# The counting of edges per node in a graph block: which one-hot is stationary and which one moves

## The chip, the core and the metric

One Trainium2 chip, one of its cores. The metric is the device time of one execution of the program in microseconds (us), the median over several runs.

## What is computed

The reference puts four blocks behind one another on 8192 rows of 128 numbers: a leaky attention over a dense adjacency matrix, a graph block with a list of edges and four experts, a second dense attention, and a routed mixture of eight experts. The change touches only the preparation of the second block, in which edges are sorted by the node that they lead to:

```
src = concatenate([edge_index[0], loops]); dst = concatenate([edge_index[1], loops])
e_max = segment_max(e, dst, num_segments=M)
denom = segment_sum(ee, dst, num_segments=M)
agg = segment_sum(msg, dst, num_segments=M)
```

The list has 524288 edges. To sort them by `dst`, the kernel first counts how many edges lead to each of the 8192 nodes.

## The kernel before, in words

The program is a chain of phases; each phase is a block in which every engine has its own instruction list, and a block ends when all engines have ended theirs. The first three phases are in `sort_and_project`. "pack" reads the edges and squeezes the wanted ones to the left of each of 128 partitions; "count" (lines 626 to 711) counts them per node; "place" (from line 714) gives each edge its place in the sorted list. The attention follows.

A node number is written as 64 * part + offset: part is one of P = 128, offset one of NF = 64. The edges stand in columns of 128, one edge on each partition. A group is GC = 8 columns. For a group, VectorE builds two arrays of ones and zeros in bf16 with `one_hots_across` (lines 932 to 935): the offset one-hots OF (128 partitions x 64 x 8; first instruction, line 934) and the part one-hots OP (128 x 128 x 8; second instruction, line 935). The group's column number is the innermost index of both arrays, so that `OF[:, :, c]`, one column's one-hots, is a read of 64 elements that lie 8 bf16 elements, 16 bytes, apart, and `OP[:, :, c]` one of 128 elements that lie 16 bytes apart.

TensorE then multiplies, for each of the 8 columns, one one-hot against the other and adds the product to one table in PSUM. The table has an entry for every pair (part, offset). There are two tables, counted one after the other: HISTC from OPC and OFC (edges of one special source, loop at lines 695 to 700, 112 groups in the profiled execution) and HIST from OP and OF (the other edges, loop at lines 703 to 708, 38 groups). Before and behind each loop a matmul with a tile `zero` opens or closes the accumulation (lines 694, 701, 702, 709). No matmul is left out for an empty column.

The order is held by semaphores. The one-hots have two buffers. VectorE may build group g when the matmuls of group g - 2 have ended (`counted`, `same_counted`); TensorE may start on group g when its second one-hot is built (`hot`, `same_hot`). The opening matmul adds 2 to `counted`, so that VectorE can't build for the second table before the first one is closed. Behind the loops VectorE copies HISTC to `repeat` (line 671), adds 1 to HIST for the loop edge of each node (line 674), sums it (line 675), gets a prefix over the partitions through one TensorE matmul (line 711) and works out the starts of the nodes' ranges. Beside this, SyncE's queue clears the tensor `runs` in DRAM (line 651); ScalarE does nothing and GpSimd only one memset.

In the phase "place" four kinds of matmul matter for the reading of the rows. Line 872 adds the product of `OP[b][:, :, c]` (stationary) and `OF[b][:, :, c]` (moving) to a table, with the same spacing of elements as in "count". Line 849 has the stationary `OP[b][:, :, c]` with 16 bytes between elements, and the moving 128 x 128 identity, whose elements are adjacent. Lines 855 and 856 have a broadcast column stationary and adjacent elements moving, and accumulate in pairs on one place in PSUM.

Of the kernel before, what the change touches and what calls it, by code (L numbers as in the profile page):

```python
# [8 lines left out]
ALU = mybir.AluOpType  # L9
# [9 lines left out]
P = 128  # L19
BANK = 512  # L20
# [219 lines left out]
def sort_and_project(nc, ident, edge_index, N, rec, plan, self_idx, self_rec, ctl, endi, cont, repeat, runs,  # L240
# [14 lines left out]
    NF = N // P  # L255
# [10 lines left out]
    with Phase(nc, "sort") as ph:  # L266
# [356 lines left out]
        with Phase(nc, "count") as pc:  # L623
            OF = [pc.sbuf(f"OF{k}", [P, NF, GC], BF16) for k in range(2)]
            OP = [pc.sbuf(f"OP{k}", [P, P, GC], BF16) for k in range(2)]
            w = pc.sbuf("w", [P, 8, NF])
            wi = pc.sbuf("wi", [P, NF], I32)
            tot = pc.sbuf("tot", [P, 2])
            zero = pc.sbuf("zero", [P, P], BF16)
            OFC = [pc.sbuf(f"OFC{k}", [P, NF, GC], BF16) for k in range(2)]  # L630
            OPC = [pc.sbuf(f"OPC{k}", [P, P, GC], BF16) for k in range(2)]
            HIST = pc.psum("hist", [P, BANK])
            HISTC = pc.psum("histc", [P, BANK])
            BASE = pc.psum("base", [P, BANK])
            hot, counted, hist_ok, tot_ok, base_ok, dve_step, zero_ok = pc.sems(
                "hot", "counted", "hist_ok", "tot_ok", "base_ok", "dve_step", "zero_ok")
            same_hot, same_counted, same_ok = pc.sems("same_hot", "same_counted", "same_ok")
            runs_clear, runs_out = pc.sems("runs_clear", "runs_out")
            clear = pc.sbuf("clear", [P, CHUNK, runs.shape[1]])
            HC = CE // 2  # L640
            with nc.Block() as block:
                @block.gpsimd
                def _(pool):
                    nc.gpsimd.memset(clear[:], 0.0).then_inc(runs_clear, 1)

                @block.sync
                def _(sp):
                    rows = runs.rearrange("(p t) c -> p t c", p=P)
                    sp.wait_ge(runs_clear, 1)
                    with sp.Fori(0, LMAX // CHUNK) as i:  # L650
                        sp.dma_start(rows[:, bass.ds(i * CHUNK, CHUNK), :], clear[:]).then_inc(runs_out, 16)
                    sp.wait_ge(runs_out, 16 * (LMAX // CHUNK))

                @block.vector
                def _(dve):
                    groups = dve.value_load(ctl[0:1, 0:1], min_val=1, max_val=CE // (2 * GC))
                    same_groups = dve.value_load(ctl[0:1, 3:4], min_val=1, max_val=HC // GC)
                    nc.vector.memset(zero[:], 0.0).then_inc(zero_ok, 1)
                    with dve.Fori(0, same_groups) as i:
                        for b in range(2):  # L660
                            dve.wait_ge(same_counted, 2 * i + b + 1)
                            cols = bass.ds(i * GC + b * HC, GC)
                            one_hots_across(nc, OFC[b], OPC[b], value, offC[:, cols], partC[:, cols], NF, GC)[1].then_inc(same_hot, 1)
                    with dve.Fori(0, groups) as i:
                        for b in range(2):
                            dve.wait_ge(counted, 2 * i + b + 1)
                            cols = bass.ds((2 * i + b) * GC, GC)
                            one_hots_across(nc, OF[b], OP[b], value, offB[:, cols], partB[:, cols], NF, GC)[1].then_inc(hot, 1)
                    step = Chain(dve, dve_step)
                    dve.wait_ge(same_ok, 1)  # L670
                    step(nc.vector.tensor_copy(repeat[:], HISTC[:, 0:NF]))
                    dve.wait_ge(hist_ok, 1)
                    c1, incl, start, last = w[:, 0, :], w[:, 1, :], w[:, 2, :], w[:, 3, :]
                    step(nc.vector.tensor_scalar(c1, HIST[:, 0:NF], 1.0, None, ALU.add))
                    step(nc.vector.tensor_reduce(tot[:, 0:1], c1, AX.X, ALU.add))
                    dve.sem_inc(tot_ok, 1)
                    dve.wait_ge(base_ok, 1)
                    step(nc.vector.tensor_copy(tot[:, 1:2], BASE[:, 0:1]))
                    step(nc.vector.tensor_tensor_scan(incl, c1, c1, tot[:, 1:2], ALU.add, ALU.max))
                    step(nc.vector.tensor_tensor(start, incl, c1, ALU.subtract))  # L680
                    step(nc.vector.tensor_scalar(start1[:], start, 1.0, None, ALU.add))
                    step(nc.vector.tensor_scalar(last, incl, -1.0, None, ALU.add))
                    step(split_rows(nc, step, start, Lc[:, 0:1], Lc[:, 1:2], Lc[:, 2:3], Lc[:, 3:4], wi[:], w[:, 4, :], w[:, 5, :], w[:, 6, :], self_idx[:]))
                    step(split_rows(nc, step, last, Lc[:, 0:1], Lc[:, 1:2], Lc[:, 2:3], Lc[:, 3:4], wi[:], w[:, 4, :], w[:, 5, :], w[:, 6, :], endi[:]))

                    step(nc.vector.scalar_tensor_tensor(out=w[:, 7, :], in0=w[:, 6, :], scalar=Lc[:, 2:3], in1=start, op0=ALU.mult, op1=ALU.add))
                    step(nc.vector.tensor_scalar(cont[:], w[:, 7, :], 0.0, None, ALU.is_lt))

                @block.tensor
                def _(pe):  # L690
                    groups = pe.value_load(ctl[0:1, 0:1], min_val=1, max_val=CE // (2 * GC))
                    same_groups = pe.value_load(ctl[0:1, 3:4], min_val=1, max_val=HC // GC)
                    pe.wait_ge(zero_ok, 1)
                    nc.tensor.matmul(HISTC[:, 0:NF], zero[:], zero[:, 0:NF], start=True, stop=False, skip_group_check=True).then_inc(same_counted, 2)
                    with pe.Fori(0, same_groups) as i:
                        for b in range(2):
                            pe.wait_ge(same_hot, 2 * i + b + 1)
                            for c in range(GC):
                                ins = nc.tensor.matmul(HISTC[:, 0:NF], OPC[b][:, :, c], OFC[b][:, :, c], start=False, stop=False, skip_group_check=True)
                            ins.then_inc(same_counted, 1)  # L700
                    nc.tensor.matmul(HISTC[:, 0:NF], zero[:], zero[:, 0:NF], start=False, stop=True, skip_group_check=True).then_inc(same_ok, 1)
                    nc.tensor.matmul(HIST[:, 0:NF], zero[:], zero[:, 0:NF], start=True, stop=False, skip_group_check=True).then_inc(counted, 2)
                    with pe.Fori(0, groups) as i:
                        for b in range(2):
                            pe.wait_ge(hot, 2 * i + b + 1)
                            for c in range(GC):
                                ins = nc.tensor.matmul(HIST[:, 0:NF], OP[b][:, :, c], OF[b][:, :, c], start=False, stop=False, skip_group_check=True)
                            ins.then_inc(counted, 1)
                    nc.tensor.matmul(HIST[:, 0:NF], zero[:], zero[:, 0:NF], start=False, stop=True, skip_group_check=True).then_inc(hist_ok, 1)
                    pe.wait_ge(tot_ok, 1)  # L710
                    nc.tensor.matmul(BASE[:, 0:1], tri[:], tot[:, 0:1], start=True, stop=True).then_inc(base_ok, 1)


        with Phase(nc, "place") as pp:
            OF = [pp.sbuf(f"OF{k}", [P, NF, GC], BF16) for k in range(2)]
            OP = [pp.sbuf(f"OP{k}", [P, P, GC], BF16) for k in range(2)]
# [215 lines left out]
def one_hots_across(nc, off_hot, part_hot, value, off, part, NF, GC):  # L932

    return (nc.vector.tensor_tensor(off_hot[:], value[:, 0:NF, :], off.unsqueeze(1).to_broadcast([P, NF, GC]), ALU.is_equal),
            nc.vector.tensor_tensor(part_hot[:], value[:], part.unsqueeze(1).to_broadcast([P, P, GC]), ALU.is_equal))
# [1851 lines left out]
def graph_network(nc, x, adj, L0_gnn_W, L0_gnn_a, L0_ffn_W_gat, L0_ffn_att_src, L0_ffn_att_dst, L0_ffn_b_gat,  # L2787
# [28 lines left out]
    with Phase(nc, "top") as top:  # L2816
# [12 lines left out]
        low = top.sbuf("low", [P, 1])  # L2829
        levels = top.sbuf("levels", [1, 1], I32)  # L2830
        sort_and_project(nc, ident, L0_ffn_edge_index, N, rec, plan, self_idx, self_rec, ctl, endi, cont, repeat, runs,
                         x, L0_gnn_W, L0_gnn_a, H, rows0, WD, srow, scol, dcol, low, levels)
        wide = top.sbuf("X", [P, T + 4, D])
# [40 lines left out]
```

## Time and profile before

| what | value |
|---|---|
| median of three runs | 4454.92 us |
| lowest and highest | 4442.82 and 4462.66 us |
| span of the profiled execution, first to last instruction | 4090.2 us |
| median of the runs minus that span | 364.7 us |
| phase "count", first matmul to the last one of the loops | 414.7 to 597.6 us of the span |

The profiled execution's time with what lies around it was not recorded apart; its span is all of it that the profile gives. All changes of a phase are therefore worked out within the span and added to the median of the runs.

The page of the profile gives for each engine its busy time, and in 40 slices of about 102 us how busy it was. PE is TensorE's matmuls, PEld its loads of stationary operands, DVE VectorE. In the lists of instructions, "128*128 128x64" on a matmul means 128 rows by 128 columns of stationary operand and 64 moving columns. The ends of matmuls are modelled, so the distance from start to start is the better measure of what a matmul costs in a stream.

### The profile page before, as it was taken

How to read it: one execution, taken by the hardware profiler on the slowest of the kernel's cores; microseconds unless marked ns; L12 is line 12 of the kernel's file. 1: busy time of each engine (PE TensorE's matmuls, PEld its weight loads, DVE VectorE, ACT ScalarE, POOL GpSimd, SP SyncE). 2: the span in 40 equal slices, each digit the busy share in tenths (PEclk: the TensorE clock that was granted, in tenths of full speed). 3: DMA queues.
4: the chain of work that ended last, by engine and by line, in shares of the span. 5: the costliest groups of instructions: out<-in, count | busy, mean ns of one | idle time of the engine just before them, and what ended most of it. 6: DMA issues, size and time to landing. Idle time of an engine off the chain costs nothing. (4 is left out here: it accounts for less than half of the span.)

```text
span 4090.2 us, 62225 instructions
## 1 busy us (share of the span) xinstructions
PE 2990.8 (73%) x17446; PEld 1902.2 (47%) x17446; DVE 2628.1 (64%) x5711; ACT 1614.7 (39%) x2876; POOL 1166.2 (29%) x1158
## 2 busy tenths in 40 slices
PE   0300879839999999999954887101599999977994
PEld 0300768725555555555533555001466666644663
DVE  9999779968888888888884222237734444442333
ACT  5301005527777777777753555101400010012221
POOL 0000005047777400000002777760001211213442
PEclk9999999969999999999985999555599999988997
DMA  3200940058878878777741222133233333323446
GB/s 136 72 0 0 371 163 12 0 195 281 290 273 288 294 269 288 284 279 289 282 145 22 73 73 69 33 96 103 98 102 108 114 103 108 113 63 125 129 124 187
DMA packets 278617, 619.23 MB, mean 151 GB/s; under 512 B 74673, under 2 KB 117816, under 8 KB 277374
## 3 DMA queue, kind: packets, MB, share of 16 engines
q1 hardware_dynamic: 211446, 502.44, 37.0%
q10 hardware_dynamic: 32200, 92.89, 5.7%
q0 software_dynamic: 34880, 22.97, 2.9%
q14 instruction: 68, 0.56, 0.0%
q8 instruction: 23, 0.38, 0.0%
HBM read 434.17 MB, written 185.82 MB: 152 GB/s over the span
## 5 line engine op out<-in xcount | busy, mean ns | idle before, releaser
L1749 PE MATMUL at_out<-at_pt,top_H 128*128 128x512 f32 x2048 | 995.1, 608 | 54.7 <-DVE at_turned L1669 46.4
L1591 ACT ACTIVATE at_rl<-at_qrow,at_less,at_steep 128x512 f32<-128x512 f32 x1024 | 746.5, 805 | 8.7 <-DVE at_turned L1669 8.6
L1973 PE MATMUL at_out<-at_parts,at_a 128*128 128x387 bf16 x4096 | 686.1, 328 | 15.7 <-DVE at_parts L2046 15.7
L1676 DVE SCALAR_TENSOR_TENSOR at_pt<-at_rl,at_turned 128x1024 f32<-128x1024 f32 x512 | 608.9, 1218 | 15.7 <-ACT at_rl L1591 15.7
L1973 PEld LDWEIGHTS at_out<-at_parts,at_a 128*128 128x128 fp8e4 x4096 | 399.7, 98 | 289.0 <-issue 17.9
L1669 DVE CAST at_turned<-at_tp 128x1024 uint8<-128x1024 f32 x322 | 393.5, 1222 | 172.7 <-PE at_tp L1740 170.7
L1749 PEld LDWEIGHTS at_out<-at_pt,top_H 128*128 128x128 f32 x2048 | 349.3, 191 | 309.3 <-issue 301.8
L1740 PEld LDWEIGHTS at_tp<-at_identS,at_adj 128*128 128x128 fp8e4 x4128 | 274.9, 98 | 302.2 <-issue 302.2
L921 POOL DMA_INDIRECT rec<-at_part x304 | 381.6, 1255 | 103.7 <-issue 85.9
L1073 POOL DMA_INDIRECT runs_GT<-tab,runs_RC x352 | 338.3, 961 | 115.9 <-issue 105.5
L1740 PE MATMUL at_tp<-at_identS,at_adj 128*128 128x128 bf16 x4128 | 316.1, 220 | 9.1 <-DMA at_adj<-in_adj_dram 8.4
L1921 POOL DMA_INDIRECT slots<-at_Y,at_dest x128 | 123.5, 965 | 634.0 <-DVEq L2151 597.9
L1598 ACT CAST at_turned<-at_tp 128x1024 uint8<-128x1024 f32 x192 | 193.8, 1009 | 223.3 <-PE at_tp L1740 223.3
L1065 POOL DMA_INDIRECT runs_firstg<-tab,runs_firsti x2 | 2.0, 985 | 828.3 <-DVEq L1092 828.0
L2424 PE MATMUL ex_hp<-ex_XS,ex_WB 128*128 128x512 f32 (+1 forms) x472 | 217.2, 596 | 1.9 <-DMA ex_WB<-wts 1.9
L2530 POOL DMA_INDIRECT y<-ex_YS,ex_to x156 | 151.5, 971 | 201.3 <-DVE ex_YS L2511 161.5
L1128 DVE TENSOR_TENSOR runs_own<-runs_GT,runs_flag 128x64 f32<-128x64 f32 x22 | 6.8, 308 | 312.5 <-DMA runs_GT<-tab,runs_RC 312.5
L2008 ACT ACTIVATE at_small<-at_small 128x4 f32<-128x4 f32 x16 | 3.3, 205 | 500.8 <-DVEq L2104 500.8
L2490 DVE TENSOR_TENSOR ex_HH<-ex_SU,ex_hp 128x512 f32<-128x512 f32 (+1 forms) x118 | 80.8, 685 | 163.2 <-ACT ex_SU L2468 163.2
L2468 ACT ACTIVATE ex_SU<-ex_hp 128x512 f32<-128x512 f32 (+1 forms) x118 | 70.4, 596 | 235.1 <-PE ex_hp L2424 235.1
L1227 PEld LDWEIGHTS runs_yp<-runs_down,runs_HH 128*128 128x128 f32 x1024 | 144.9, 219 | 17.8 <-issue 15.6
L1216 PE MATMUL runs_hp<-top_H,runs_up 128*128 (+1 forms) x256 | 125.9, 616 | 30.4 <-DVEq L1110 30.4
(591 smaller groups left out, 4470.4 us busy)
## 6 DMA issues: line engine op xcount, KB each, us to landing
at_adj<-in_adj_dram SPq DMA_DIRECT2D x516, 512.0 KB
adjT<-at_turned ACTq DMA_DIRECT2D x128, 512.0 KB, 5.2
at_a<-adjT SPq DMA_DIRECT2D x128, 512.0 KB, 3.6
runs<-count_clear SPq DMA_DIRECT2D x131, 384.0 KB, 4.0
ex_WB<-wts SPq DMA_DIRECT2D x42, 533.0 KB, 3.6
y<-runs_YS ACTq DMA_DIRECT2D x65, 256.0 KB, 2.1
f_YB<-y SPq DMA_DIRECT2D x16, 1024.0 KB, 11.4
ex_SL<-slots SPq DMA_DIRECT2D x42, 260.0 KB, 3.6
```

The lines of the kernel that those rows point to most:

```text
L921: pool.indirect_dma_start(rec, bass.IndirectOffsetOnAxis(ap=part[h][:, c, 2:3], axis=0), part[h][:, c, 0:2], None, bounds_check=LAST, oob_ ...
L1073: pool.indirect_dma_start(GT[b][:, c, :], None, tab, bass.IndirectOffsetOnAxis(ap=RC[b][:, c, 1:2], axis=0)).then_inc(gt_in[b], 16)
L1227: ins = nc.tensor.matmul(YP[:, x % 2, q * D:(q + 1) * D], HH[x % 2][k][:, q * P:(q + 1) * P], down[:, x, k, :], start=False, stop=(q == GQ ...
L1591: ins = nc.scalar.activation(RL[v % NBUF][:, k, :], qrow[:], ACT.Relu, bias=less[:], scale=steep[:, u:u + 1])
L1598: nc.scalar.copy(AT[c % NAT][:, 2 * (v % VC):2 * (v % VC) + 2, :], TP[v % 2][:]).then_inc(copied[0], 1)
L1669: nc.vector.tensor_copy(AT[c % NAT][:, 2 * (v % VC):2 * (v % VC) + 2, :], TP[v % 2][:]).then_inc(copied[1], 1)
L1676: nc.vector.scalar_tensor_tensor(out=PT[v % NBUF][:], in0=RL[v % NBUF][:], scalar=1.0, in1=AT[v // VC % NAT][:, 2 * (v % VC):2 * (v % VC) ...
L1740: ins = nc.tensor.matmul(TP[v % 2][:, k, t * P:(t + 1) * P], bits[c % NBUF][:, t, o:o + P, 0], identS[:], start=True, stop=True)
L1749: ins = nc.tensor.matmul(OUT[:], H[:, u, :], PT[v % NBUF][:, k, :], start=(u == 0), stop=(u == T - 1))
L1973: ins = nc.tensor.matmul(OUT[:, g, x, 0:3 * D1], ones[c % NBUF][:, j, x * P:(x + 1) * P], parts[:, u].rearrange("p k d -> p (k d)"), start ...
L2424: ins = nc.tensor.matmul(HP[0:n, k, s, :], WB[b][:, w:w + n], XS[b][:], start=True, stop=True)
L2530: pool.indirect_dma_start(y, bass.IndirectOffsetOnAxis(ap=to[b][:, q:q + 1], axis=0), YS[b][:, q, :], None, bounds_check=2 * N - 1, oob_is ...
```

## The change

In both loops and in the four opening and closing matmuls the operands change places. The offset one-hots (64 columns) become stationary, the part one-hots (128 columns) move. The tables lie on 64 partitions by 128 columns in place of 128 by 64. At the end each table is copied to SBUF (`lying`), turned by a TensorE transpose into a new PSUM tile (`TURN`), and read from there. Two semaphores for each way are added. The builds on VectorE, the groups, the buffers and their waits stay.

```diff
+            TURN = pc.psum("turn", [P, 2, BANK])
+            lying = pc.sbuf("lying", [NF, 2, P])
+            lies, stands = [pc.sem(f"lies{k}") for k in range(2)], [pc.sem(f"stands{k}") for k in range(2)]
...
                     dve.wait_ge(same_ok, 1)
-                    step(nc.vector.tensor_copy(repeat[:], HISTC[:, 0:NF]))
+                    nc.vector.tensor_copy(lying[:, 0, :], HISTC[0:NF, 0:P]).then_inc(lies[0], 1)
                     dve.wait_ge(hist_ok, 1)
+                    nc.vector.tensor_copy(lying[:, 1, :], HIST[0:NF, 0:P]).then_inc(lies[1], 1)
+                    dve.wait_ge(stands[0], 1)
+                    step(nc.vector.tensor_copy(repeat[:], TURN[:, 0, 0:NF]))
+                    dve.wait_ge(stands[1], 1)
                     c1, incl, start, last = w[:, 0, :], w[:, 1, :], w[:, 2, :], w[:, 3, :]
-                    step(nc.vector.tensor_scalar(c1, HIST[:, 0:NF], 1.0, None, ALU.add))
+                    step(nc.vector.tensor_scalar(c1, TURN[:, 1, 0:NF], 1.0, None, ALU.add))
...
                             for c in range(GC):
-                                ins = nc.tensor.matmul(HISTC[:, 0:NF], OPC[b][:, :, c], OFC[b][:, :, c], start=False, stop=False, skip_group_check=True)
+                                ins = nc.tensor.matmul(HISTC[0:NF, 0:P], OFC[b][:, :, c], OPC[b][:, :, c], start=False, stop=False, skip_group_check=True)
...
-                    nc.tensor.matmul(HISTC[:, 0:NF], zero[:], zero[:, 0:NF], start=False, stop=True, skip_group_check=True).then_inc(same_ok, 1)
-                    nc.tensor.matmul(HIST[:, 0:NF], zero[:], zero[:, 0:NF], start=True, stop=False, skip_group_check=True).then_inc(counted, 2)
+                    nc.tensor.matmul(HISTC[0:NF, 0:P], zero[:, 0:NF], zero[:], start=False, stop=True, skip_group_check=True).then_inc(same_ok, 1)
+                    nc.tensor.matmul(HIST[0:NF, 0:P], zero[:, 0:NF], zero[:], start=True, stop=False, skip_group_check=True).then_inc(counted, 2)
...
                             for c in range(GC):
-                                ins = nc.tensor.matmul(HIST[:, 0:NF], OP[b][:, :, c], OF[b][:, :, c], start=False, stop=False, skip_group_check=True)
+                                ins = nc.tensor.matmul(HIST[0:NF, 0:P], OF[b][:, :, c], OP[b][:, :, c], start=False, stop=False, skip_group_check=True)
...
-                    nc.tensor.matmul(HIST[:, 0:NF], zero[:], zero[:, 0:NF], start=False, stop=True, skip_group_check=True).then_inc(hist_ok, 1)
+                    nc.tensor.matmul(HIST[0:NF, 0:P], zero[:, 0:NF], zero[:], start=False, stop=True, skip_group_check=True).then_inc(hist_ok, 1)
+                    for k in range(2):
+                        pe.wait_ge(lies[k], 1)
+                        nc.tensor.transpose(TURN[:, k, 0:NF], lying[:, k, :], ident[0:NF, 0:NF]).then_inc(stands[k], 1)
```

## Rows read from the trace of the kernel before

**Rows 1.** Windows of "count": us, busy us of each engine (instructions), granted clock, DMA share, GB/s.

```profile
414.50:551.00 136.50, 119.55 (x897) 102.13 (x898) 110.75 (x225) 0.00 (x0) 0.00 (x0) 1.00 0.97 378
551.00:598.00 47.00, 41.11 (x309) 34.66 (x307) 38.13 (x77) 0.00 (x0) 0.00 (x0) 1.00 0.00 0
```

**Rows 2.** Waits between 415 and 600 us: us in total, times, longest.

```profile
DVE count_OFC L934 <- PE count_histc L699: 24.2, 55, 0.5
PE count_histc L699 <- DVE count_OPC L935: 16.7, 56, 1.3
```

**Rows 3.** Timeline of two pairs of groups: start us, us, engine, line, xcount, idle before.

```profile
450.02 2.14 PE L699 MATMUL count_histc<-count_OFC,count_OPC 128*128 128x64 bf16 x16 [0.29 <-DVE count_OPC L935]
...
451.35 0.43 DVE L934 TENSOR_TENSOR count_OFC<-sort_value,sort_both 128x512 bf16<-128x512 bf16 x1 [0.45 <-PE count_histc L699]
451.70 0.68 DVE L935 TENSOR_TENSOR count_OPC<-sort_value,sort_both 128x1024 bf16<-128x1024 bf16 x1
452.30 0.43 DVE L934 TENSOR_TENSOR count_OFC<-sort_value,sort_both 128x512 bf16<-128x512 bf16 x1
...
452.44 0.81 PE L699 MATMUL count_histc<-count_OFC,count_OPC 128*128 128x64 bf16 x5 [0.28 <-DVE count_OPC L935]
```

**Rows 4.** Instructions on the two tables: ns min/median/max, first and last start in us.

```profile
L699 PE MATMUL count_histc<-count_OFC,count_OPC x896: 293/302/327, 416.2 to 550.9; 128*128 128x64 bf16 x180
L707 PE MATMUL count_hist<-count_OF,count_OP x304: 293/302/325, 552.6 to 597.6; 128*128 128x64 bf16 x152
```

**Rows 5.** Timeline of the passage from the first table to the second.

```profile
551.05 0.23 PE L701 MATMUL count_histc<-count_zero 128*128 128x64 bf16 x1
551.10 0.23 PE L702 MATMUL count_hist<-count_zero 128*128 128x64 bf16 x1
```

**Rows 6.** Timeline of the start of "place", stationary read at 16 bytes, moving elements adjacent.

```profile
612.08 1.07 PE L849 MATMUL place_tb<-place_identB,place_OP 128*128 128x128 bf16 x8 [5.21 <-DVE place_OP L775]
```

**Rows 7.** Line 849 up to 616.2 us and behind it: ns min/median/max, starts.

```profile
L849 PE MATMUL place_tb<-place_identB,place_OP x8: 311/311/323, 612.1 to 612.8; 128*128 128x128 bf16 x8
L849 PE MATMUL place_tb<-place_identB,place_OP x304: 219/226/236, 616.4 to 808.7; 128*128 128x128 bf16 x152
```

**Rows 8.** Line 872 up to 616.2 us and behind it: ns min/median/max, starts.

```profile
L872 PE MATMUL place_hr<-place_OF,place_OP x3: 297/301/316, 614.6 to 616.0; 128*128 128x64 bf16 x3
L872 PE MATMUL place_hr<-place_OF,place_OP x300: 287/316/322, 616.0 to 809.5; 128*128 128x64 bf16 x150
```

**Rows 9.** Timeline of TensorE in "place" at 614 and at 700 us.

```profile
614.43 0.31 PE L855 MATMUL place_dd<-place_identF,sort_partB 128*128 128x128 bf16 x1
614.54 0.31 PE L856 MATMUL place_dd<-place_identB,sort_offB 128*128 128x128 bf16 x1
614.65 0.30 PE L872 MATMUL place_hr<-place_OF,place_OP 128*128 128x64 bf16 x1
614.77 0.62 PE L876 MATMUL place_lk<-place_HS,place_OPT 128*128 128x64 f32 x2
...
699.79 0.42 PE L849 MATMUL place_tb<-place_identB,place_OP 128*128 128x128 bf16 x4
700.07 0.31 PE L872 MATMUL place_hr<-place_OF,place_OP 128*128 128x64 bf16 x1
...
700.41 0.22 PE L855 MATMUL place_dd<-place_identF,sort_partB 128*128 128x128 bf16 x1
700.46 0.22 PE L856 MATMUL place_dd<-place_identB,sort_offB 128*128 128x128 bf16 x1
```

**Rows 10.** Timeline of the end of "count".

```profile
595.74 2.14 PE L707 MATMUL count_hist<-count_OF,count_OP 128*128 128x64 bf16 x16 [0.26 <-DVE count_OP L935]
...
596.57 0.22 DVE L671 COPY top_repeat<-count_histc 128x64 f32<-128x64 f32 x1
...
597.71 0.23 PE L709 MATMUL count_hist<-count_zero 128*128 128x64 bf16 x1
598.05 0.23 DVE L674 TENSOR_SCALAR count_w<-count_hist 128x64 f32<-128x64 f32 x1 [1.26 <-PE count_hist L709]
598.31 0.22 DVE L675 TENSOR_REDUCE count_tot<-count_w 128x1 f32<-128x64 f32 x1
...
598.64 0.58 PE L711 MATMUL count_base<-count_tot,sort_tri 128*128 128x1 f32 x2 [0.70 <-DVEq L676]
599.27 0.16 DVE L678 COPY count_tot<-count_base 128x1 f32<-128x1 f32 x1 [0.73 <-PE count_base L711]
```

**Rows 11.** Two single f32 transposes: a stationary operand of 64 and of 128 columns.

```profile
L610 PEld LDWEIGHTS pack_st<-top_ident,top_scol x1: 129/129/129, 310.6 to 310.6; 128*64 128x64 f32 x1
L610 PE MATMUL pack_st<-top_ident,top_scol x1: 422/422/422, 310.6 to 310.6; 128*64 128x128 f32 x1
L587 PEld LDWEIGHTS pack_ms<-top_ident,sort_both x1: 182/182/182, 11.8 to 11.8; 128*128 128x128 f32 x1
```

More of the change, by code:

```diff
@@ L693, in _ @@
                     pe.wait_ge(zero_ok, 1)
-                    nc.tensor.matmul(HISTC[:, 0:NF], zero[:], zero[:, 0:NF], start=True, stop=False, skip_group_check=True).then_inc(same_counted, 2)
+                    nc.tensor.matmul(HISTC[0:NF, 0:P], zero[:, 0:NF], zero[:], start=True, stop=False, skip_group_check=True).then_inc(same_counted, 2)
                     with pe.Fori(0, same_groups) as i:
```

## Prediction, made before the changed kernel ran

> **What bounds the kernel now.** I read the page's slices first, to find when the edited lines run, and then looked only at "count". The windows show it as some 183 us in which ScalarE and GpSimd do nothing and neither TensorE nor VectorE is busy all the time: 119.6 and 110.8 us of the first 136.5 us [rows 1]. The only DMA there clears a tensor and has ended before the second table is counted, where the share falls from 0.97 to 0.00 [rows 1]; a phase ends when its slowest engine does, so that every microsecond added to the counting is added to the span.
>
> The waits show that the two engines wait for each other in turn, once in each pair of groups (55 and 56 times) [rows 2]. The timeline shows why. In the pair shown, TensorE starts at 450.02 and issues 16 matmuls in 2.14 us; the last one lasts 0.302 us [rows 4], so that starts are (2.14 - 0.302) / 15 = 0.1225 us apart, call it 0.12 us [rows 3]. The eighth starts at 450.02 + 7 x 0.12 = 450.86 and ends at about 451.16; VectorE's next build starts at 451.35, some 0.2 us later, lasts until 451.70 + 0.68 = 452.38, and TensorE goes on at 452.44 [rows 3]. So the pair's period of 2.42 us is the round trip of one buffer: build 1.03 + signal 0.06 + matmuls 0.84 + 0.30 + signal 0.19 = 2.42. TensorE alone would need 16 x 0.12 = 1.92 us. VectorE alone would need 2 x 0.95 = 1.90 us, from its starts at 451.35 and 452.30 [rows 3]. The kernel runs 56 + 19 = 75 such pairs. The two loops last from 416.2 to 551.05 and from 552.56 to 597.71 us, together 134.8 + 45.2 = 180.0 us [rows 4, 5, 10].
>
> **What a matmul costs here.** The change halves the stationary columns and doubles the moving ones, so everything hangs on which of the two sets the 0.12 us. I compared four kinds of matmul.
>
> First, 64 moving columns of adjacent elements: the closing and opening matmuls start 0.05 us apart and last 0.23 us [rows 5]. The counting ones, with 64 moving columns 16 bytes apart, take 0.12 us and last 0.302 us: about 0.07 us more in each measure. So adjacent reading runs at 0.05 / 64 = 0.8 ns a column, and the difference must come from the operands' spacing, stationary or moving.
>
> Second, a stationary operand of 128 columns 16 bytes apart, with 128 adjacent moving columns (line 849): eight matmuls in 1.07 us, so (1.07 - 0.311) / 7 = 0.108 us apart [rows 6, 7]. That is what 128 adjacent moving columns cost at that time, whatever the stationary operand is, for lines 855 and 856, with a broadcast column, are 0.11 us apart too [rows 9]. Later on the same line is (0.42 - 0.226) / 3 = 0.065 us apart [rows 7, 9]. So a load of 128 spaced columns needs at most 0.065 us, half of the 0.12 us, and hides behind a matmul.
>
> Third, line 872, which has the operands of the counting. It lasts 301 ns up to 616.2 us and 316 ns behind it, while line 849 falls from 311 to 226 ns [rows 7, 8]. The next matmul starts 0.12 us after it [rows 9], although it stands alone and nothing of its own kind is before or behind it. So this is no hazard of accumulating on one PSUM place again and again (lines 855 and 856 accumulate in pairs 0.05 us apart at 700.41 [rows 9]), and it isn't paced by TensorE's clock. What is left is the reading of the moving operand: about 0.12 us for 64 elements, 1.9 ns for each.
>
> On the clock: between 614 and 700 us, with no change of form, the distance of lines 855 and 856 falls from 0.11 to 0.05 us [rows 9], the ratio of the two levels of 1.2 and 2.4 GHz. The granted clock is given as 1.00 throughout "count" [rows 1], but the 0.23 us of the opening matmul's 64 columns against 0.226 us for 128 columns at 700 us [rows 5, 7] fit the lower level; I take that record as silent before 616 us. For my sum it does not matter, since line 872 shows that the spaced read is no faster at the higher level.
>
> The Trainium skill has a rule on this ("SBUF — State Buffer", in its note on cachelines): lines are of 16 bytes, and reads that go to a new line each time are penalised, which for bf16 begins at a step of 8 elements. That is this layout, the trace agrees (0.12 against 0.05 us), and it speaks against the change, for the change makes the longer of the two spaced operands the moving one. The rule that speaks for it is in "TensorE: Matmul & The Clock Gate", section "LDWEIGHTS (loading the stationary operand)": a load takes its columns / 1.2 ns, 107 ns for 128 and 53 ns for 64, by which 0.12 us would be mostly the load. The 0.065 us of line 849 speaks against that. The same page ties the fast load of weights to 128 of them, so that the new load of 64 loses it; by the page that load is then 53 ns.
>
> **The sum, part by part.**
>
> 1. Moving columns from 64 to 128, all spaced: start to start from 0.12 to 2 x 0.12 = 0.24 us, and the duration from 0.30 to 0.42 us. Bounds: from below, of the 0.302 us only what exceeds the in-stream matmul's fixed part counts as read; that part is 311 - 107 = 204 ns for line 849 [rows 7, 9], which leaves 98 ns for 64 columns, 1.53 ns each, and 0.196 us for 128. From above, line 872 at the higher clock: 316 - (226 - 65) = 155 ns, 2.4 ns a column, 0.31 us for 128. I take 0.24 because the stream itself, the nearest row, shows it without any fixed part taken off.
>
> 2. The stationary operand from 128 to 64 columns: its load is hidden now and stays hidden behind 0.24 us. No row has a 64-column bf16 load; an f32 one takes 129 against 182 ns [rows 11]. Even at 1.9 ns a column, 0.12 us, it is covered. Value: nothing. Were it not covered, it would cost up to 0.12 us each (third rival).
>
> 3. The loop. The round trip of a buffer becomes 1.03 + 0.06 + 7 x 0.24 + 0.42 + 0.19 = 3.38 us, but TensorE alone needs 16 x 0.24 = 3.84 us for a pair. So TensorE becomes the bound, and VectorE, done 0.46 us ahead, waits for it. Each pair takes 3.84 us in place of 2.42 (2.40 on the mean). All 1200 matmuls: 1200 x 0.24 = 288.0 us in place of 180.0: **+108.0 us**. VectorE's 150 builds don't change, and nothing else is in the phase to be covered by the longer loops: the clearing DMA ends earlier than them.
>
> 4. Openings and closings, each table: the last matmul's drain is 0.12 us longer. Twice: +0.2 us.
>
> 5. The turn at the end. The second table's chain gets a copy from PSUM, about 0.25 us (128x64 takes 0.22 us [rows 10]; this one is 64x128), and a trip to TensorE and back with an f32 transpose: between 598.53, where the sum on line 675 ends, and 599.27 the like trip takes 0.74 us with 0.58 us of matmul [rows 10], against 0.42 us for a single transpose [rows 11]. So 0.25 + 0.74 + a little for the second semaphore: +1.0 us. The first table's copy and transpose, and the copy to `repeat` (0.22 us), lie within these waits; the copy to `repeat`, queued on VectorE ahead of line 674, waits only for the first transpose, which TensorE does before the second table's copy is done. Bounds of this part: 0.7 to 1.5 us.
>
> Sum: 108.0 + 0.2 + 1.0 = **+109 us**. The span goes from 4090.2 to about 4199 us. The median of the runs lies 364.7 us above the span, and nothing in the change touches what is around it: 4454.9 + 109 = **4564 us**, 2.4% slower. By the bounds of part 1 the loops need 1200 x 0.196 = 235 us (TensorE's 3.14 us a pair is then hardly above the round trip of 3.04) or 1200 x 0.31 = 372 us: +56 and +193 us with parts 4 and 5, that is 4511 and 4648 us.
>
> **The rivals.**
>
> First: the load sets the pace, and the moving spaced read costs little. Then the halved load goes away as the bound and matmuls are paced by 128 columns at 0.107 us with a duration of 0.311 us as on line 849 [rows 7]. The round trip: 1.03 + 0.06 + 0.75 + 0.31 + 0.19 = 2.34 us against 2.42. That is -0.08 x 75 = -6 us, +1 us for the turn: 4450 us, within the noise. For it: the counting's loads and matmuls both have spaced operands, and no row has a spaced moving operand with an adjacent stationary one. Against it: line 849's 0.065 us with the same load. It needs a load of over 0.107 us. If in addition the clock went to its higher level (distance 0.05, duration 0.22 [rows 9]), the round trip would be 1.03 + 0.06 + 0.35 + 0.22 + 0.19 = 1.85 us, VectorE's 1.90 us would bound, and (2.40 - 1.90) x 75 = 37 us would be won: 4419 us. This is the case that ends on the other side.
>
> Second: loads and moving reads share one supply of spaced reads. 128 + 64 = 192 elements cost 0.12 us now, and 64 + 128 = 192 cost the same after: nothing but the turn, 4456 us. For it: 0.12 / 192 gives 0.63 ns, and line 849's 0.065 us for 128 spaced elements gives 0.5 ns, not far from it. Against it: line 872 has its next load beside it in adjacent f32 and still takes 0.12 us.
>
> Third: the new load of 64 columns isn't hidden: it comes at 0.12 us (1.9 ns a column) on top of the 0.24. Then 1200 x 0.36 = 432 us, +253 us: 4708 us. Against it: loads hide now in every stream that I looked at. It decides only if spaced reads of both operands exclude each other, which the 0.12 us of today leaves no room for at 0.065 + 0.12.
>
> That the change doesn't do what it says isn't likely: the operands are exchanged in both loops, and nothing depends on data.
>
> **How the numbers follow.** Forecast 0.82; first rival 0.06 within its 6 us and 0.03 with the faster clock; second 0.04; third 0.05. The median of the three runs scatters by some 20 us, so 0.5% (22 us) is about what can be told from no change. Slower by more than that: 0.82 + 0.05 = 0.87. Same: 0.06 + 0.04 = 0.10. Faster: 0.03. The range holds the forecast with nearly the whole of part 1's bounds, 4510 to 4640; the rivals outside have 0.18 together.
>
> **What would show it.** In the profile after, lines 699 and 707 (moved down by a few lines) should be 0.24 us apart and last about 0.42 us; TensorE should have no idle time in the loops except at their starts, and VectorE should wait for it some 1.9 us in each pair, in both groups; the stretch from the first to the last counting matmul should be near 290 us; the time from the last closing matmul to line 675's successor should be 1 us longer. A distance near 0.12 us would show the second rival, 0.107 us or less the first, 0.36 us the third. I am wrong if the distance does not scale with the moving columns, or if the spaced read is slowed today by the load beside it and gets faster with the smaller one.

## The result, and the profile after

| | before | after | ratio, 95% interval |
|---|---|---|---|
| median, first comparison | 4448.87 us | 4539.88 us | 1.0232 [1.0191, 1.0273] |
| median, second comparison (a faster chip) | 4095.21 us | 4194.81 us | 1.0235 [1.0206, 1.0265] |

The changed kernel is slower by 91 us between the medians of the first comparison, by 0.0232 x 4448.87 = 103 us by its ratio, and by 99.6 us in the second. Neither interval holds 1. The prediction was +109 us, 4564 us.

Windows of the counting in the changed kernel (columns as in [rows 1]):

```profile
414.50:622.00 207.50, 206.18 (x896) 174.09 (x897) 114.88 (x224) 0.00 (x0) 0.00 (x0) 1.00 0.64 248
622.00:694.00 72.00, 70.77 (x309) 59.41 (x307) 39.09 (x77) 0.00 (x0) 0.00 (x0) 1.00 0.00 0
```

TensorE is busy for 206.2 of 207.5 us, where it was for 119.6 of 136.5 [rows 1]. VectorE is busy for 154.0 us over both windows, where it was for 148.9. The waits, over both loops, now have one direction:

```profile
DVE count_OFC L944 <- PE count_histc L706: 90.0, 110, 1.4
DVE count_OF L944 <- PE count_hist L714: 29.8, 36, 1.4
...
PE count_histc L706 <- DVE count_OPC L945: 1.3, 1, 1.3
PE count_hist L714 <- DVE count_OP L945: 1.2, 1, 1.2
```

TensorE waits once for each table, at its start. VectorE waits before 110 groups of 112 and 36 of 38, 0.82 us each time. Before, each engine waited once in a pair [rows 2]. The instructions on the first table, and where the loops end:

```profile
L706 PE MATMUL count_histc<-count_OPC,count_OFC x896: 405/409/481, 416.1 to 622.0; 128*64 128x128 bf16 x180
...
L708 PE MATMUL count_histc<-count_zero x1: 287/287/287, 622.3 to 622.3; 128*64 128x128 bf16 x1
```

A matmul lasts 409 ns instead of 302 [rows 4]. From 416.1 to 622.3 us are 206.2 us for 896 matmuls: 0.230 us from start to start. The second table takes from 623.9 to 693.9 us, 70.0 us for 304, the same pace. The loops take 276.2 us in place of 180.0: +96 us. The end of the phase, from the timeline:

```profile
693.86 0.29 PE L716 MATMUL count_hist<-count_zero 128*64 128x128 bf16 x1
694.07 0.18 PEld L719 LDWEIGHTS count_turn<-top_ident,count_lying 64*128 64x128 f32 x1 [0.29 <-issue]
694.07 0.81 PE L719 MATMUL count_turn<-top_ident,count_lying 64*128 64x64 f32 x2
694.18 0.28 DVE L676 COPY count_lying<-count_hist 64x128 f32<-64x128 f32 x1 [2.46 <-PE count_hist L716]
694.48 0.23 DVE L678 COPY top_repeat<-count_turn 128x64 f32<-128x64 f32 x1
...
695.00 0.23 DVE L681 TENSOR_SCALAR count_w<-count_turn 128x64 f32<-128x64 f32 x1 [0.30 <-PE count_turn L719]
```

From the closing matmul's start to the instruction that adds 1 are 1.14 us, where it was 598.05 - 597.71 = 0.34 [rows 10]: the turn costs 0.8 us. The passage from the first table to the second takes 623.87 - 622.25 = 1.62 us in place of 1.51. Together: +97 us within "count".

### The profile page after: what moved, and what is told of

It is laid out like the page before. It is cut to its first block and busy times, and to the rows that moved or that the text cites. A ratio compares the mean times of both kernels' runs of the same rounds, so it can differ in the third digit from the quotient of the medians.

```text
span 4558.5 us, 62231 instructions
## 1 busy us (share of the span) xinstructions
PE 3214.6 (71%) x17448; PEld 2075.7 (46%) x17448; DVE 2633.6 (58%) x5713; ACT 1613.0 (35%) x2876; POOL 1132.4 (25%) x1158
## 5 line engine op out<-in xcount | busy, mean ns | idle before, releaser
L1759 PE MATMUL at_out<-at_pt,top_H 128*128 128x512 f32 x2048 | 1015.1, 619 | 95.4 <-DVE at_turned L1679 48.8
L931 POOL DMA_INDIRECT rec<-at_part x304 | 355.8, 1170 | 103.7 <-issue 95.2
L1152 DVE TENSOR_TENSOR runs_sum_in<-runs_GT,runs_sum_in 128x256 f32<-128x256 f32 x22 | 17.2, 783 | 431.1 <-ACT runs_decay L1175 412.1
L706 PE MATMUL count_histc<-count_OPC,count_OFC 128*64 128x128 bf16 x896 | 206.3, 409 | 1.3 <-DVE count_OPC L945 1.3
L706 PEld LDWEIGHTS count_histc<-count_OPC,count_OFC 128*64 128x64 bf16 x896 | 174.0, 194 | 33.4 <-DVE count_OPC L945 1.4
L1226 PE MATMUL runs_hp<-top_H,runs_up 128*128 (+1 forms) x256 | 142.5, 670 | 52.6 <-DVEq L1120 30.4
```

Of the source, the lines that this page charges most:

```text
L706: ins = nc.tensor.matmul(HISTC[0:NF, 0:P], OFC[b][:, :, c], OPC[b][:, :, c], start=False, stop=False, skip_group_check=True)
L931: pool.indirect_dma_start(rec, bass.IndirectOffsetOnAxis(ap=part[h][:, c, 2:3], axis=0), part[h][:, c, 0:2], None, bounds_check=LAST, oob_ ...
L1759: ins = nc.tensor.matmul(OUT[:], H[:, u, :], PT[v % NBUF][:, k, :], start=(u == 0), stop=(u == T - 1))
```

## The experiments

The theory: in these loops a matmul's pace is set by the reading of its moving operand, whose elements are 16 bytes apart. The change doubles that operand. The rivals: the load of the stationary operand sets the pace; both reads share one supply; part of the loss comes elsewhere. Except where noted, an experiment changes only the counting.

**The kernel before, unchanged.** The profiled executions of before and after differ by 4558.5 - 4090.2 = 468 us, of which only 97 lie in "count".

> The kernel before, unchanged, to see how its parts spread from one profiled execution to the next. Both theories: the two counting loops again take 180 us in all, with 0.12 us from matmul to matmul. The profiled executions of before and after differ by 468 us in span though only 96 us of that lie in the counting; if that rest has nothing to do with the change, this run's span lies near 4450 us rather than at 4090 us, with the phase 'place' near 300 us and the graph block near 540 us as in the profile after. If the rest came with the change, the span is near 4090 us.

This one execution took 4438.73 us, with a span of 4437.0 us. Its counting is that of the first profile: 302 ns, and loops of 135.1 + 45.2 = 180.3 us.

```profile
L699 PE MATMUL count_histc<-count_OFC,count_OPC x896: 293/302/326, 416.3 to 551.3; 128*128 128x64 bf16 x180
```

The rest of the difference lies behind, in the same code. Windows of "place" and of the graph block, first of the first profile of before, then of this run:

```profile
598.00:811.00 213.00, 190.17 (x1850) 161.50 (x1851) 200.18 (x1395) 107.55 (x457) 61.39 (x62) 1.00 0.06 20
2224.00:2564.00 340.00, 263.38 (x1310) 187.18 (x1311) 75.63 (x279) 179.18 (x283) 256.65 (x267) 0.89 0.27 67
```

```profile
598.00:895.00 297.00, 207.47 (x1856) 181.26 (x1854) 201.84 (x1401) 107.40 (x457) 60.06 (x62) 0.80 0.04 14
2359.00:2890.00 531.00, 310.88 (x1309) 202.49 (x1310) 75.04 (x287) 175.62 (x280) 260.14 (x276) 0.76 0.16 43
```

The same instructions take 297 and 531 us in place of 213 and 340. The busy times of VectorE, ScalarE and GpSimd are nearly unchanged; TensorE's grow by 9% and 18%, at a lower granted clock (0.80 in place of 1.00, 0.76 in place of 0.89), and the rest is waiting. The kernel before is thus 9% slower on one chip than on another: its medians were 4479 us on this run's chip and 4095 us on two others. The first profile came from an execution of the latter kind, while its times are of the former. So the 364.7 us that I put "around the span" are nothing of the sort: here time and span differ by 1.7 us. Why these phases depend on the chip was not followed up; the change has no part in it, as the next run shows.

**The changed kernel again, on a chip of the faster kind.**

> The changed kernel once more, beside the kernel before, because the profiled executions of before and after differed by 350 us outside the counting. Theory: the change costs 276 - 180 = 96 us in the loops and 1 us in the turn whatever the rest of the execution is like: 97 us more than the kernel before on the same chip, ratio 1.022 to 1.024. Rival (part of the loss comes later, as a lower granted clock in 'place' that the change brings about): clearly more than 97 us, or another difference where the rest runs faster.

4194.81 against 4095.21 us: +99.6 us, ratio 1.0235 [1.0206, 1.0265]; loops 276.2 us to the tenth. The span of its profile is 4187.2 us, 97.0 us above the 4090.2 of the first profile of before, all of it in "count". The loss is the same where the rest runs 350 us shorter. Its windows behind the counting are those of the first profile of before:

```profile
694.00:909.00 215.00, 191.23 (x1856) 161.87 (x1854) 201.71 (x1407) 107.57 (x457) 61.27 (x62) 1.00 0.06 20
2324.00:2663.00 339.00, 262.74 (x1311) 184.25 (x1312) 75.36 (x279) 179.59 (x284) 255.82 (x268) 0.89 0.26 67
```

**The moving columns cut in two, with 64 stationary ones.**

```diff
-    ins = nc.tensor.matmul(HIST[0:NF, 0:P], OF[b][:, :, c], OP[b][:, :, c], ...)
+    for m in range(2):
+        half_of = slice(m * (P // 2), (m + 1) * (P // 2))
+        ins = nc.tensor.matmul(HIST[0:NF, half_of], OF[b][:, :, c], OP[b][:, half_of, c], ...)
```

> The changed kernel, with each matmul's 128 moving columns cut into two matmuls of 64 columns behind loads of the same 64 stationary columns: twice as many matmuls, the same table. Theory (the spaced moving read sets the pace, 1.68 ns a column, with some 15 ns for each matmul on top): 0.122 us from start to start, the loops at 16 x 2 x 0.122 = 3.90 us a pair, 293 us in all. Proportional to the columns with nothing fixed: 0.115 us, 276 us in all. Rival, the pace of before came from loading 128 spaced columns: 0.06 to 0.10 us, 150 to 240 us in all. Rival, loads and moving reads share one supply (192 elements in 0.12 us): 128 elements, 0.08 us, 192 us in all.

```profile
L708 PE MATMUL count_histc<-count_OPC,count_OFC x1792: 299/299/368, 416.4 to 631.4; 128*64 128x64 bf16 x200
```

1792 matmuls in 631.4 - 416.4 = 215.0 us: 0.120 us each, between the two forms that I had put, with 64 stationary columns, where 128 stationary columns gave 0.1225. Half the load changes the pace by 2%. This ends the first rival (0.06 to 0.10) and the shared supply (0.08). The two loops took 288 us, and the one execution 4603.26 us beside a median of 4479.31 for the kernel before. It also sizes my term: two matmuls of 64 columns take 0.240 us and one of 128 takes 0.230. Read as a straight line, that is 0.010 us for each matmul and (0.230 - 0.120) / 64 = 1.72 ns for each column.

**The moving columns cut in two, in the kernel before.** The same edit, on the kernel before: two matmuls of 32 columns behind 128 stationary ones.

> The kernel before, with each matmul's 64 moving columns cut into two matmuls of 32, each behind a load of the same 128 spaced stationary columns. Theory (1.68 ns a moving column and 15 ns fixed): 0.069 us from start to start if the load of 128 columns, at most 0.065 us on line 849, stays hidden; then a pair's round trip grows by 15 x 0.069 + 0.25 against 7 x 0.122 + 0.30, that is by 0.13 us, the loops take about 190 us in all. Rival, the load of 128 spaced columns sets the pace of before: 0.12 us from start to start still, TensorE alone 3.84 us a pair, 288 us in all.

Timeline of two pairs of groups:

```profile
447.82 2.25 PE L701 MATMUL count_histc<-count_OFC,count_OPC 128*128 128x32 bf16 x32 [0.29 <-DVE count_OPC L939]
450.30 2.26 PE L701 MATMUL count_histc<-count_OFC,count_OPC 128*128 128x32 bf16 x32 [0.23 <-DVE count_OPC L939]
```

(2.25 - 0.24) / 31 = 0.065 us on the mean, as 0.010 + 32 x 1.72 ns = 0.065 gives from the other two sizes. But this mean holds the first step behind each wait, 0.087 to 0.089 us; most of the other steps are 0.060 to 0.067 us, with a median of 0.061, hardly above half of the 0.120 us for 64 columns. So the fixed 0.010 us rests on the step from 64 to 128 columns alone. The loops took 182 us, though every stationary operand is loaded twice; a pace set by the load would have made 288. The one execution took 4472.95 us, 6 us below the median of the kernel before.

**One operand closer at a time.** The arrays are laid out as two blocks of four columns, so that a column's elements are 8 bytes apart; the builds stay two VectorE instructions. The edit shown brings the moving one-hots alone closer; the other array keeps one block of eight columns, 16 bytes from element to element.

```diff
-    OF = [pc.sbuf(f"OF{k}", [P, NF, GC], BF16) for k in range(2)]
+    OF = [pc.sbuf(f"OF{k}", [P, GC // 4, NF, 4], BF16) for k in range(2)]
...
-    ins = nc.tensor.matmul(HIST[:, 0:NF], OP[b][:, :, c], OF[b][:, :, c], ...)
+    ins = nc.tensor.matmul(HIST[:, 0:NF], OP[b][:, c // 8, :, c % 8], OF[b][:, c // 4, :, c % 4], ...)
```

First the moving one-hots alone:

> The kernel before with only the moving one-hots (64 offset columns) laid out 8 bytes apart; the stationary ones stay 16 bytes apart. Theory (the moving read alone sets the pace): 0.055 to 0.065 us from matmul to matmul, loops near 143 to 150 us, VectorE's 1.90 us a pair being the bound. Rival (two spaced operands share one supply of reads, so the spaced load counts too): between 0.065 and 0.12 us, by 0.63 ns for each of the 128 spaced stationary elements 0.08 us or more.

Then the stationary ones alone:

> The kernel before with only the stationary one-hots (128 part columns) laid out 8 bytes apart; the moving ones stay 16 bytes apart. Theory: 0.120 us from matmul to matmul as before, loops 180 us. Rival (the load of 128 spaced columns sets the pace, or shares it): 0.06 to 0.08 us, loops 145 to 155 us.

Timelines, of the moving ones closer (from its second run, below) and of the stationary ones closer:

```profile
448.15 0.71 PE L707 MATMUL count_histc<-count_OFC,count_OPC 128*128 128x64 bf16 x8 [0.23 <-DVE count_OPC L243]
...
449.17 0.72 PE L707 MATMUL count_histc<-count_OFC,count_OPC 128*128 128x64 bf16 x8 [0.31 <-DVE count_OPC L243]
```

```profile
449.21 2.05 PE L707 MATMUL count_histc<-count_OFC,count_OPC 128*128 128x64 bf16 x16 [0.31 <-DVE count_OPC L243]
```

With the moving ones closer, (0.71 - 0.248) / 7 = 0.066 us, 248 ns each. With the stationary ones closer, (2.05 - 0.297) / 15 = 0.117 us, loops of 176 us. So the moving operand's spacing is nearly all of it; the stationary one's costs 0.005 us of the 0.1225. One execution of each gave 4062.6 and 4099.4 us beside a median of 4094.9. The first again, over four executions:

> The kernel before with the moving one-hots alone 8 bytes apart, timed: the loops take 145.6 us, 34 us less than 180; 4 us more than with both 8 bytes apart, if the loads of 16-byte spacing cost anything where the pace is VectorE's. Ratio to the kernel before 0.992.

4060.69 against 4095.21 us, ratio 0.990 [0.9872, 0.9928]. The loops took 145.6 us. Its waits show that VectorE is the bound, for it waits only at the tables' starts, and TensorE before each group:

```profile
PE count_histc L707 <- DVE count_OPC L243: 31.1, 112, 1.3
...
DVE count_OF L243 <- PE count_hist L710: 1.0, 1, 1.0
```

**Both operands closer, in the kernel before.**

> The kernel before with the one-hots of both kinds laid out so that one column's elements are 8 bytes apart instead of 16 (two groups of 4 columns each, built by the same two VectorE instructions). Theory (only a read that goes to a new 16-byte line each time is slow): 0.06 to 0.07 us from matmul to matmul, 0.24 us each, the round trip of a buffer 1.03 + 0.06 + 7 x 0.065 + 0.24 + 0.19 = 1.98 us, 75 pairs in 149 us instead of 180: 31 us faster, ratio 0.993. Rival, any spacing makes the read slow: 0.12 us still and 180 us, ratio 1.00. Rival, the 0.12 us isn't a matter of spacing at all but of accumulating on one place: 0.12 us still. If the VectorE instruction were slower in this layout, its mean (0.425 and 0.684 us before) would show it.

Ratio 0.9913 [0.9874, 0.9951], 4442.45 us; the builds kept their times (0.42 and 0.684 us). Eight matmuls take 0.66 us, (0.66 - 0.242) / 7 = 0.060 us each, though they still add to one table: accumulating on one place is not what cost the 0.12 us. Then on another chip:

> The kernel before with both one-hots 8 bytes apart, again: the loops 142 us in place of 180, so 38 us less, and about 135 us less than the changed kernel beside it. Ratio to the kernel before 0.991.

4055.00 us, ratio 0.9888 [0.986, 0.9916]; loops of 142 us in both, VectorE's 1.90 us a pair. This is the version that beats both kernels: 40 us below the one before and 140 us below the changed one beside it.

**Both operands closer, in the changed kernel.**

> The changed kernel (offset one-hots stationary, part one-hots moving, two turned tables) with both one-hots laid out 8 bytes from element to element in place of 16. Theory (the loss comes from the longer spaced operand being the moving one, and a spacing of 16 bytes alone makes it slow): 0.107 us from matmul to matmul, the pace of 128 adjacent columns on line 849 at the lower clock, about 0.29 us each; round trip 1.03 + 0.06 + 7 x 0.107 + 0.29 + 0.19 = 2.32 us, 75 pairs in 174 us, and 1 us for the turn: 5 us faster than the kernel before, ratio 1.00, and 101 us less in the loops than the changed kernel. Should TensorE be granted its higher clock: VectorE's 1.90 us a pair, 143 us. Rival (the exchange itself costs, by its tables, its load or its accumulation over 128 columns): 0.23 us still, loops 276 us, ratio 1.02.

```profile
449.46 2.07 PE L714 MATMUL count_histc<-count_OPC,count_OFC 128*64 128x128 bf16 x16 [0.31 <-DVE count_OPC L243]
```

Ratio to before 1.0007 [0.9997, 1.0017]: (2.07 - 0.298) / 15 = 0.118 us a matmul, loops of 177 us. So the rival that the exchange itself costs 0.23 us a matmul is gone. But the exchange isn't free: with both operands 8 bytes apart in either order, the loops take 177 us exchanged and 142 us unexchanged, and the kernels lie 3 us above and 40 us below the one before. I had expected 0.107 us, and 143 us for the loops should TensorE be granted its higher clock. It was granted that in part, for in this run the clock record already changes level during the loops, and the pace did not follow: the median from start to start is 0.118 us at either level. Windows at either level, and a pair of groups in each:

```profile
428.00:434.60 6.60, 5.93 (x48) 5.23 (x48) 5.36 (x13) 0.00 (x0) 0.00 (x0) 0.50 1.01 396
479.10:485.80 6.70, 5.78 (x47) 4.82 (x46) 5.68 (x12) 0.00 (x0) 0.00 (x0) 1.00 1.01 397
...
430.44 2.07 PE L714 MATMUL count_histc<-count_OPC,count_OFC 128*64 128x128 bf16 x16 [0.31 <-DVE count_OPC L243]
...
480.37 2.07 PE L714 MATMUL count_histc<-count_OPC,count_OFC 128*64 128x128 bf16 x16 [0.31 <-DVE count_OPC L243]
```

At 8 bytes, too, the read isn't paced by TensorE's clock. The last run, of the changed kernel with both one-hots 4 bytes apart (four blocks of two columns), asked for that remainder:

> The changed kernel with both one-hots 4 bytes apart. With 8 bytes a matmul of 128 moving columns took 0.117 us where adjacent columns took 0.107 us on line 849. Theory (what is left at 8 bytes is still the cost of new lines, every second read): 0.107 us at 4 bytes, the loops near 172 us. Rival (the 0.010 us comes from the load beside it or from VectorE's writing): 0.117 us still, loops near 177 us.

```profile
L714 PE MATMUL count_histc<-count_OPC,count_OFC x896: 308/308/316, 416.5 to 581.4; 128*64 128x128 bf16 x180
...
L243 DVE TENSOR_TENSOR count_OPC<-sort_value,sort_both x112: 1035/1066/1128, 415.4 to 579.5; 128x1024 bf16<-128x1024 bf16 x112
```

Eight matmuls took 1.06 us, (1.06 - 0.308) / 7 = 0.107 us: the remainder went with the spacing. Whether it was the moving operand's alone isn't shown, since both came closer and VectorE's writing changed with them. But the loops took 221 us, and the kernel 4153 us, because VectorE's build with runs of two elements takes 1066 ns in place of 684, and VectorE now sets the pace. I had not expected that, and my 172 us missed it. It was one execution, 58 us above the kernel before.

## Why the prediction was right

**The bound and the loop.** That the loop is a round trip of one buffer and becomes TensorE's was right: TensorE has no idle time but at the starts, VectorE waits in both groups. It waits 1.6 us in a pair, not the 1.9 I named: half of the difference is the pair's period, 3.68 us and not 3.84. The other half is that I took VectorE's 0.95 us for a group, its pace without gaps, where with a wait in front of each group a build counts with its full 1.03 us.

**Part 1, the moving columns: right in mechanism, 4% too large.** 0.24 us was predicted and 0.230 measured; over 1200 matmuls that is the 12 us between 288 and 276. The term was mis-sized by doubling: 128 columns cost 0.010 us less than twice 64. My "without any fixed part taken off" would explain it, but the 0.061 us between most matmuls of 32 columns speaks against a fixed part of that size, so what saves the 0.010 us stays open. Both bounds, 0.196 and 0.31, were wide of it. The sum therefore ended at 109 where 97 was within "count", and about 100 was timed.

**Part 2, the load: right.** It stays hidden, though in the profile it lasts 194 ns instead of 146. The third rival needed 0.36 us. Halving the stationary columns at 64 moving ones won 2%, so the gain that the change could have had did not exist. The Trainium skill's rule that a load takes its columns / 1.2 ns ("TensorE: Matmul & The Clock Gate", section "LDWEIGHTS (loading the stationary operand)"), 107 ns for 128, did not hold here as a pace: with 32 moving columns, 128 stationary ones were loaded every 0.065 us. Whether the fast load that the prediction names is behind this isn't shown. The Trainium skill's rule on 16-byte cachelines ("SBUF — State Buffer", in its note on cachelines) is borne out in part. At a step of 16 bytes 128 columns took 0.230 us, against 0.11 us for adjacent ones [rows 9]; but the note counts a step of 8 bf16 elements, which is this one, as still free. It also asks for two hits on a line, which a step of 8 bytes has, and there 128 columns took 0.118 us at either clock level, where adjacent ones take 0.11 us at the lower and 0.05 us at the higher [rows 9].

**Parts 4 and 5.** The later ends of the two loops' last matmuls were 0.2 us as said, the turn 0.8 us for 1.0. The copy was 0.28 us for 0.25; from its end to the next instruction were 0.54 us, where I had taken the 0.74 us of a trip with two f32 matmuls. The first table's turn and the copy to `repeat` were hidden, as said.

**The rivals.** The first (load) and second (shared supply) were told apart from the theory by the two cuts and by the closer operands: for 64 stationary and 64 moving columns they had a pace of at most 0.10 us, and it was 0.120. I argued against them from line 849 and line 872 alone, and these rows had it right.

**What I had wrong beside the sum** is the 364.7 us "around the span": it was the difference between two chips. It did no harm because the change's cost doesn't depend on the rest, but it could have, and the sign was there: a twelfth of the time would have had no instruction in it.

## What to carry to other kernels

Before exchanging stationary and moving operands, find which of the two sets a matmul's pace: compare its distance from start to start with that of other lines in the trace that share one operand's layout. A moving bf16 operand read 16 bytes from element to element costs twice an adjacent one at the lower clock (0.230 against 0.107 us for 128 columns), so the shorter of two spaced operands should be the moving one, and better still, the layout should bring the elements of a column nearer to each other. Do both: with 8 bytes, the loops took 142 us with the 64 columns moving, where VectorE set the pace, and 177 us with the 128 columns moving. At 8 bytes 128 columns lose a tenth against adjacent ones at the lower clock, but their 0.118 us is about twice what adjacent ones take at the higher (0.05 us on line 855). Check the producer too: at 8 bytes VectorE's builds kept their time; at 4 bytes the larger one took 1.56 times as long, and the kernel ended 58 us above the one before.

## What the runs showed of the hardware

- Matmuls with moving bf16 columns 16 bytes apart followed each other after 0.065, 0.120 and 0.230 us for 32, 64 and 128 columns (the first is a mean that holds the longer first step behind each wait; the median step is 0.061 us).
- The time went with the bytes passed over: 128 columns took 0.230 us at 16 bytes and 0.118 us at 8, which is 1.80 and 1.84 ns for each 16 bytes, and the 0.118 us were the same at either clock level. At 4 bytes this would be 0.059 us, an estimate from these two. Measured were 0.107 us, as for adjacent columns at the lower level.
- 128 stationary bf16 columns 16 bytes apart were loaded every 0.065 us behind 32 moving ones; from 16 to 8 bytes their spacing was worth 0.005 us of 0.1225.
- TensorE stayed at the lower of its two clock levels, 1.2 GHz, through 206 us in which it issued spaced matmuls without a gap: the closing matmul behind them has adjacent columns and lasted 287 ns, where 128 adjacent columns took 0.22 us on line 855 at 2.4 GHz [rows 9]. I had not expected a fully busy stream to stay there. With the same columns 8 bytes apart and 0.31 us of waiting in front of each pair of groups, the level changed again and again during the loops (granted clock 0.50 at 428 to 434.6 us, 1.00 at 479.1 to 485.8 us). Why is not shown. The granted clock of the changed kernel's windows says 1.00 for that stretch, which the durations contradict. By the rows it cost nothing here, since the read at 16 bytes is no faster at the higher level [rows 8].
